# A graph network kernel on one core: the first two turns of the edge stage gather from the input instead of from the stored table

## The reference

```python
# layers 0 and 1 (GINE), on h = relu(layernorm(x))
h = jnp.maximum(_layernorm(x, axis=-1), 0.0)
for l in range(2):
    msg = jax.nn.relu(h[src] + edge_attr)
    agg = jax.ops.segment_sum(msg, dst, num_segments=N_NODES)
    h = (h + agg) @ W1[l] + b1[l]
    # batch norm over the nodes, relu
    h = relu(relu(h @ W2[l] + b2[l]))
x = x + h
# layers 2 and 3 (GIN) on relu(layernorm(x)): agg = segment_sum(h[src]), two matmuls each
```

## Time and profile before

| | |
|---|---|
| median of three runs | 2903.31 us (2901.6 to 2903.5) |
| profiled execution, its own time | 2906.73 us |
| its span | 2904.8 us |
| busy: PE, DVE, ACT, POOL | 1876.1, 1609.8, 520.5, 2020.4 us |
| first gather to last gather of layer 0 | 48.93 to 1060.05 us |
| first gather to last gather of layer 1 | 1115.56 to 2136.29 us |
| layers 2 and 3 | to the end of the span |
| mean granted TensorE clock | 0.834 |

### The profile page before, as it was taken

One profiled execution on the slowest core, in us unless ns is written; L12 is line 12 of the kernel. 1 busy time (PEld: TensorE's weight loads), 2 busy tenths in 40 slices (PEclk: granted clock), 3 DMA queues, 4 the chain that ended last, 5 costly groups with the idle time before them and its releaser, 6 DMA issues.

```text
span 2904.8 us, 28601 instructions
## 1 busy us (share of the span) xinstructions
PE 1876.1 (65%) x9233; PEld 1285.7 (44%) x9233; DVE 1609.8 (55%) x1943; ACT 520.5 (18%) x584; POOL 2020.4 (70%) x2060
## 2 busy tenths in 40 slices
PE   2555565555465553555555555555567999989998
PEld 2434343434343432434343434334343666546655
DVE  6766666666666644666575656665646222352223
ACT  3111111111111122121212122222234000030001
POOL 2777777777777744777777777777734777557773
PEclk7777777777777777888788787888877999999999
DMA  5333333333333333343434344444424666466663
GB/s 168 102 116 103 122 102 116 105 120 119 119 113 125 115 104 91 116 143 116 141 123 149 122 149 136 155 138 156 142 79 152 218 208 199 152 199 211 200 203 110
DMA packets 224847, 403.61 MB, mean 139 GB/s; under 512 B 41224, under 2 KB 129116, under 8 KB 224740
## 3 DMA queue, kind: packets, MB, share of 16 engines
q1 hardware_dynamic: 159204, 267.94, 26.6%
q0 software_dynamic: 65536, 134.35, 17.2%
HBM read 337.92 MB, written 64.21 MB: 138 GB/s over the span
## 4 chain that ended last, share of the span: by engine, by line
POOL 53%; PE 25%; issue 17%; DVE 2%; ACT 1%; SPq 1%; DMA 1%; DVEq 0%; POOLq 0%; ACTq 0%
POOL xg L535 53%; PE psA L1214 17%; PE psG L1229 4%; PE psG L1278 2%; PE psA L1286 1%; PE psG L1193 1%; ACT rows_h L583 0%; SPq L411 0%; PE psG L1308 0%; DVE hid L931 0%; PE psA L1295 0%; DVE xp_room L741 0%; DVE rows_h L770 0%; DVE acc L782 0%; DMA node_table<-rows_h 0%
## 5 line engine op out<-in xcount | busy, mean ns | idle before, releaser
L535 POOL DMA_INDIRECT xg<-node_table,src_all x1568 | 1556.3, 993 | 577.1 <-issue 477.4
L1193 PE MATMUL psG<-hid,xp_room 128*128 128x160 f32 x3136 | 656.2, 388 | 792.0 <-DVE hid L824 792.0
L1193 PEld LDWEIGHTS psG<-hid,xp_room 128*128 128x128 f32 x3136 | 633.0, 264 | 835.3 <-issue 835.3
L555 POOL DMA_INDIRECT xg<-node_table,idx x480 | 461.0, 960 | 267.2 <-issue 263.4
L849 DVE TENSOR_SCALAR cell_room<-psG,cell_all 128x1960 f16<-128x1960 int16 x544 | 630.1, 1217 | 0.0
L860 DVE TENSOR_TENSOR xp_room<-xp_room,xg 128x1024 f32<-128x1024 f32 x196 | 238.5, 1217 | 667.0 <-DMA xg<-node_table,src_all 667.0
L1178 PE MATMUL psA<-cell_room,xp_room 128*128 128x512 f16 (+1 forms) x2176 | 478.4, 370 | 145.1 <-ACT count_out L593 145.1
L1178 PEld LDWEIGHTS psA<-cell_room,xp_room 128*128 128x128 f16 x2176 | 206.6, 98 | 386.4 <-ACT count_out L593 180.1
L593 ACT CAST count_out<-psA 128x1960 f16<-128x1960 f32 x96 | 172.0, 1792 | 963.9 <-PE psA L1178 963.9
L598 ACT ACTIVATE xp_room<-xp_room 128x1024 f32<-128x1024 f32 x196 | 206.2, 1057 | 715.2 <-DVE xp_room L860 715.0
L824 DVE SCALAR_TENSOR_TENSOR hid<-loc_all,round_off,psG 128x2560 f32<-128x2560 f32 x98 | 280.4, 2861 | 0.1
(11 more groups left out here) (128 smaller groups left out, 615.0 us busy)
## 6 DMA issues: line engine op xcount, KB each, us to landing
xp_room<-in_edge_attr_dram SPq DMA_DIRECT2D x98, 768.0 KB, 4.7
cell_room<-count_store SPq DMA_DIRECT2D x16, 3000.0 KB
count_store<-count_out SPq DMA_DIRECT2D x96, 490.0 KB, 3.1
hid<-count_store SPq DMA_DIRECT2D x16, 2880.0 KB
xp_room<-in_edge_attr_dram SPq DMA_DIRECT2D x98, 256.0 KB, 5.0
xg<-node_table,src_all POOLq DMA_INDIRECT x1568
node_table<-rows_h SPq DMA_DIRECT2D x48, 256.0 KB, 2.3
xg<-node_table,idx POOLq DMA_INDIRECT x480
```

Of the source, the lines that this page charges most:

```text
L535: nc.gpsimd.indirect_dma_start(xg[:, n % 2, u, j, :], None, table, bass.IndirectOffsetOnAxis(ap=src_all[:, s, j:j + 1], axis=0),).then_inc ...
L555: nc.gpsimd.indirect_dma_start(xg[:, q, u, j, :], None, table, bass.IndirectOffsetOnAxis(ap=idx[:, q, u, j:j + 1], axis=0),).then_inc(row_ ...
L1193: last = nc.tensor.matmul(psG[:, q, h * WIN:(h + 1) * WIN], ea[:, t, u, j, :], hot[:, q, u, j, :], start=(u == slots[0] and j == 0), stop= ...
```

## The change

Turns 0 and 1 of layer 0 gather rows of the input `x` itself, with the same indices. POOL therefore no longer waits for the stored table before them; that wait stands before turn 2 now. The gathered rows still lack layer norm and relu, so both are done on the gathered tiles. For each of the two turns DVE takes the statistics of the 16 gathered chunks (`raw_statistics`), ACT takes the square root and applies relu with the negative mean as bias in place (`centre_raw`), and DVE multiplies by the reciprocal deviation and adds the edge attributes chunk by chunk (`raw_sums`), in place of the two halves of L860. The small results lie in a free part of `hid`. Nothing changes from turn 2 on.

```diff
+RAW_TURNS = 2
+RAW_CHUNKS = SLOTS * EPP
...
             for layer in range(2):
-                pool.wait_ge(table_written, 16 * GROUPS * (layer + 1))
+                if layer == 1:
+                    pool.wait_ge(table_written, 16 * GROUPS * 2)
                 for n in range(layer * TURNS, (layer + 1) * TURNS):
+                    if n == RAW_TURNS:
+                        pool.wait_ge(table_written, 16 * GROUPS)
...
-                                xg[:, n % 2, u, j, :], None, table,
+                                xg[:, n % 2, u, j, :], None, x if n < RAW_TURNS else table,
...
+            def centre_raw(n):
+                act.wait_ge(raw_var_ready, n + 1)
+                act.activation(raw_rstd, raw_var, ACT.Sqrt, bias=small_eps[:, 0:1]).then_inc(raw_std_ready, 1)
+                for u in range(SLOTS):
+                    for j in range(EPP):
+                        c = u * EPP + j
+                        last = act.activation(xg[:, n, u, j, :], xg[:, n, u, j, :], ACT.Relu, bias=raw_neg_mean[:, c:c + 1])
+                    last.then_inc(raw_centred, 1)
...
+            centre_raw(0)
             act.wait_ge(weights_turned, 1)
             for k in range(4):
...
+            centre_raw(1)
             act.wait_ge(params_loaded, PARAMS)
...
+            def raw_statistics(n):
+                for h in range(WINDOWS):
+                    dve.wait_ge(gathered[n][h], 16 * EPP * len(HALVES[h]))
+                for u in range(SLOTS):
+                    for j in range(EPP):
+                        last = nc.vector.bn_stats(raw_stats[:, u * EPP + j, :], xg[:, n, u, j, :])
+                link(last)
+                mean = lambda k: raw_stats[:, :, 3 * k + 1]
+                sq = lambda k: raw_stats[:, :, 3 * k + 2]
+                nc.vector.tensor_tensor(raw_tmp[:, 0, :], mean(0), mean(1), ALU.add)
+                nc.vector.tensor_tensor(raw_tmp[:, 1, :], mean(0), mean(1), ALU.subtract)
+                link(nc.vector.tensor_tensor(raw_tmp[:, 2, :], sq(0), sq(1), ALU.add))
+                nc.vector.tensor_scalar(raw_neg_mean, raw_tmp[:, 0, :], -0.5, None, ALU.mult)
+                link(nc.vector.scalar_tensor_tensor(out=raw_var, in0=raw_tmp[:, 1, :], scalar=0.25,
+                                                    in1=raw_tmp[:, 1, :], op0=ALU.mult, op1=ALU.mult))
+                nc.vector.scalar_tensor_tensor(out=raw_var, in0=raw_tmp[:, 2, :], scalar=1.0 / D,
+                                               in1=raw_var, op0=ALU.mult, op1=ALU.add).then_inc(raw_var_ready, 1)
+
+            def raw_sums(n):
+                dve.wait_ge(raw_std_ready, n + 1)
+                nc.vector.reciprocal(raw_rstd, raw_rstd).then_inc(raw_step, 1)
+                dve.wait_ge(raw_step, n + 1)
+                dve.wait_ge(ea_loaded[n], 32)
+                for u in range(SLOTS):
+                    dve.wait_ge(raw_centred, n * SLOTS + u + 1)
+                    for j in range(EPP):
+                        c = u * EPP + j
+                        last = nc.vector.scalar_tensor_tensor(
+                            out=ea[:, n, u, j, :], in0=xg[:, n, u, j, :], scalar=raw_rstd[:, c:c + 1],
+                            in1=ea[:, n, u, j, :], op0=ALU.mult, op1=ALU.add)
+                    if u in (HALVES[0][-1], HALVES[1][-1]):
+                        last.then_inc(summed, 1)
...
                     count_cells(n)
-                    dve.wait_ge(ea_loaded[n % RING], 32 * (n // RING + 1))
-                    for h, slots in enumerate(HALVES):
+                    if n >= RAW_TURNS:
+                        dve.wait_ge(ea_loaded[n % RING], 32 * (n // RING + 1))
+                    for h, slots in enumerate(HALVES if n >= RAW_TURNS else ()):
...
             norm_rows(0)
+            raw_statistics(0)
...
+            raw_sums(0)
             for h, rows in halves:
                 dve.wait_ge(loc_turned, h + 1)
...
             nc.vector.tensor_copy(plan_i[:, 0:1], plan_f[:, 1:2]).then_inc(rounds_ready, 1)
+            raw_statistics(1)
...
+            raw_sums(1)
             dve.wait_ge(flag_turned, 1)
             nc.vector.tensor_copy(use_counts[:, :], psA[:, 2, 0:1]).then_inc(flag_ready, 1)
```

More of the change, by code:

```diff
@@ L183, in gnn_kernel @@
         cell_shift_f = hid[0:1, 8 * SUP + 2 * CHUNKS:8 * SUP + 3 * CHUNKS]
+        RAW0 = 8 * SUP + 3 * CHUNKS + SUPERS
+        raw_stats = hid[:, RAW0:RAW0 + 6 * RAW_CHUNKS].rearrange("p (c k) -> p c k", k=6)
+        raw_tmp = hid[:, RAW0 + 6 * RAW_CHUNKS:RAW0 + 9 * RAW_CHUNKS].rearrange("p (k c) -> p k c", k=3)
+        raw_neg_mean = hid[:, RAW0 + 9 * RAW_CHUNKS:RAW0 + 10 * RAW_CHUNKS]
+        raw_var = hid[:, RAW0 + 10 * RAW_CHUNKS:RAW0 + 11 * RAW_CHUNKS]
+        raw_rstd = hid[:, RAW0 + 11 * RAW_CHUNKS:RAW0 + 12 * RAW_CHUNKS]
         chunk_stat = sb("chunk_stat", [P, 2, 2 * EPP])
@@ L319, in gnn_kernel @@
         out_written = sem("out_written")
+        raw_var_ready = sem("raw_var_ready")
+        raw_std_ready = sem("raw_std_ready")
+        raw_centred = sem("raw_centred")
+        raw_step = sem("raw_step")
         gathered = [[sem(f"gathered{q}_{h}") for h in range(WINDOWS)] for q in range(2)]
```

## The result

| | before | changed |
|---|---|---|
| median of ten runs each | 2903.4 us (2901.27 to 2913.81) | 2894.93 us (2885.37 to 2898.08) |
| mean of these ten | 2905.0 us | 2892.9 us |
| profiled execution, span | 2904.8 us | 2892.4 us |

The ratio is 0.9958, with a 95% interval of 0.9944 to 0.9972, so the change gains 12 us (8 to 16). The medians alone are 8.5 us apart. The forecast was 22, with a time of 2881 in a range of 2874 to 2890. The sign and the mechanism are right, the size is not, and the median lies outside the range.

A forecast was written before the change was run, and what follows sets the result against it. POOL's back-to-back gathers in layers 0 and 1 were taken as the bound. A 34 us lead, cut by a stall of some 11 us before turn 4, was to gain 22.3 us: 2903.3 - 22.3 = 2881.0, range 2874 to 2890.

The forecast's parts named there:

- the rival on the slower side: Gathers hold back DVE's two-operand operations in the prologue; at worst 20 us slower, 2923; chance 0.04.
- whoever issues first: Port rule for DVE with two SBUF inputs against GpSimd: the first to issue has the pair, the other fully blocks.
- The held gather of 84.04: Layer 0 gather taking 2.04 us, starting while L860 of 84.05 to 85.25 runs; read as agreeing with the port rule.
- The data are there: At turn 0's statistics in DVE's prologue: last gather starts at 33.5 and is usable at 36.1, so no wait.
- my sum: Start of turn 1's last raw gather on POOL: 14.0 + 31 x 1.25 + 2.0 = 54.8.
- raw_sums(1): Turn 1's 16 short sums in DVE's prologue, 0.22 us each, and 0.3 for the reciprocal: 3.8 us.
- The windows of turn 0 with turn 1's counting: Piece of DVE's list after `clear_windows`: 10.1 us, ending at 95.3.
- Statistics with the unit tables: In DVE's prologue: turn 1's statistics 4.5 us, to 61.8, and unit tables 7.3 us, to 69.1.
- `use_counts` to `clear_windows`: Piece of DVE's prologue from L1073 to the end of `clear_windows`: 12.3 us, ending at 85.2.
- the turn-1 windows: Windows of turn 1 and counting of turn 2 on DVE's list: 11.7 us, ending at 107.0.
- From there the turns run as before, only earlier.: From turn 5 of layer 0 on, no further stall; layers 1 to 3 untouched, keeping the 22.3 us gain.
- The rival with a gain of 10 to 17 us: Loads, landings or DVE-ACT hand-overs cost DVE's prologue 5 to 12 us more; 2886 to 2893; chance 0.22.

The follow-up runs named there:

- reordered: The changed kernel with each raw step moved to where its data have long landed; ratio 0.9954 to the kernel before.
- load early: The changed kernel with the load of turn 0's edge attributes moved ahead of the weights; ratio 0.9959 to the kernel before.
- store late: The changed kernel with the table's stores waiting until all of turn 0's raw gathers have landed; ratio 0.9975 to the kernel before.

## Why the forecast came out too large

**The mechanism held up to turn 4.** POOL's gathers are the bound, the head start is handed on to DVE's prologue, DVE's arrival at turn 2's add sets turn 4, and POOL stalls once. The runs that move that add move turn 4 with it: in the changed kernel, reordered, load early and store late, turn 4 starts 1.5 us behind it (110.7, 106.7, 109.7 and 113.8). Turn 5 had no stall. Gathers held VectorE by a few hundredths of a microsecond at most. L923 took 1201 to 1292 ns, and the 32 short sums took 342 to 351 ns each, with 0.26 to 0.27 us from one start to the next in both blocks. So the rival on the slower side is out. The Trainium skill's "whoever issues first" (SBUF — State Buffer, "Who interferes with whom") is borne out in one direction and not in the other. Where the add was running first, the gather waited for its end. Where the gather was first, nobody waited: in the trace of before, 114 adds start 0.12 us or more after a gather that is still running, and they took 1201 to 1227 ns and those gathers 940 to 953. The held gather of 84.04, which the prediction took as agreeing, starts 0.01 us ahead of its add; gathers that start up to 0.1 us ahead of an add are sometimes held.

**The failed step: "The data are there".** I took 2.57 us from a gather's start to its use, from the quiet end of the layer. In the prologue it was 8.4 us for turn 0 (32.75 to 41.14) and 6.7 us for turn 1 (53.25 to 59.95). The first is the edge load at 32.56, as the run with the load earlier shows. In the chain to turn 4 only the later wait counts: the second statistics started at 59.95, not 57.3, which is 2.6 us. Had the first landed in time, DVE would have waited for the second (load early: turn 4 moved by 0.8 us). The 6.7 us of turn 1 have two parts. The gather itself was held for 1.6 us by the sums of turn 0, about as long as it had started ahead of my sum (53.25 against 54.8). From its end to the use of its rows it took 4.1 us, where the quiet case has 1.6. That this second part is due to the stores and the loads of turns 1 and 2 beside it is likely, but no run takes them away.

**Mis-sized terms.** `raw_sums(1)` took 4.5 us from 71.46 to 75.93, not 3.8. The sums overlap by 0.08 us, as the statistics do, but one of them is 0.35 us long and not 0.29, so the pitch (4.29 / 16) is 0.27 and not 0.22. The windows of turn 0 with turn 1's counting took 11.6 us (87.70 to 99.33), not 10.1: the idle times of 1.17 and 0.52 us around the first L844, in which DVE's queue loads the window starts into registers, had been covered by the two adds and now stand bare. They are a cost of removing the adds. Statistics with the unit tables, `use_counts` to `clear_windows`, and the turn-1 windows were 0.3 to 0.5 us cheaper each. Together with the 2.6 us of the failed step that is 3.7 us at turn 4, 112.1 instead of 108.5. The lead there is 19.9 us by the means of three traces (18.7 by the first pair), where 22.3 was forecast.

**"From there the turns run as before, only earlier."** This held within about 1 us for layer 0, by the means: the lead at its last gather is 18.9 us, and the gathers of turns 4 and later were held for 34.0 us against 33.0. In the first pair it cost 2.9 us, and layer 0's last gather started at 1044.3 where 1038 was forecast. The spread of before's own traces is as large, so no regular loss is shown.

**What stays open.** The spans of the three traces differ by 18.9 us on average (2907.5 against 2888.6), but the timed runs by 12.1 (means of ten each) and 11.5 (medians of the second session). The traced executions are not typical ones. Those of the changed kernel took 2894.2, 2889.2 and 2887.9 us, and the second was the fastest of its five by 9 us; those of before took 2906.7, 2908.6 and 2912.7, where before's medians in these sessions were 2903.4, 2907.3 and 2904.3. So 12 us is the gain and 18.9 flatters it. The failed step and the mis-sized terms explain 3.7 us of the 10 that are missing from the forecast's 22.3, or of the nearly 14 by the medians. The rest is presumably lost behind turn 4, since the start of turn 4 repeats within 0.3 us in three traces, but in executions that were not traced, and I did not find where. From turn 4 to the end, single traces of either kernel differ by 5 to 6 us, in held gathers and in the stages between layers (52.5 to 56.1 us between layers 0 and 1). Whether the changed kernel meets the slower kind more often than before can't be told from three traces of each. The rival with a gain of 10 to 17 us, which had 0.22, is right in its number by the mean. Of its causes the late landing is there, but with 2.6 us of its 5 to 12. The range ended at a gain of 13, and the median of ten lies 5 us beyond it.

**The better version.** The changed kernel with the counting begun two turns later is 31 us faster than before and 19 faster than the changed kernel of the same session (medians 2881.66 and 2900.15). With the raw steps reordered as well it was 26 us faster than before. Both beat the two kernels.

## What to carry to other kernels

A head start given to the engine that bounds a stage lasts only until the next hand-over to an engine that did not start earlier; work forward to the first wait whose releaser stands behind the whole prologue, and lighten what stands ahead of that release. Here moving 14 us of count building behind it brought 12 us more at that point, on top of the 20 of the change. And take a transfer's latency from a stretch with the traffic that it will meet, not from a quiet one: the same gather took 2.5 us alone and 8 behind a 1 MB load.

## What the runs showed of the hardware

- A gather that starts while a VectorE operation with two SBUF operands runs waits for that operation's end, and ends 0.82 us after it. In the trace of before this accounts for 143 of the 144 gathers of more than 0.97 us (the other one is the first).
- Behind a run of sixteen short operations without a gap it can wait for the whole run: in the changed kernel the gather at 53.25 took 2.58 us and ended 0.8 us after the last sum at 55.01, while the one before it, 51.84, took 1.10. I had priced such a gather at 0.2 us.
- Some operations with one SBUF operand hold a gather too. In the changed kernel this gather ends 0.82 us after the cast:

```profile
45.16 0.42 DVE L1077 CAST hid<-hid 128x512 f32<-128x512 int32 x1
45.28 1.12 POOL L550 DMA_INDIRECT xg<-in_x_dram,src_all  x1 [0.30 <-issue]
```

- An indirect gather of 128 rows lands 2.5 us after its start in a quiet stretch, 3.5 to 5.3 beside other loads and stores, and 5 to 8 right behind a 1 MB load on another queue, by the landing records of the first 48 gathers of the changed kernel.
